# First combine tile of a soft-MoE layer: batch 1's first lower half ahead of the row maxima, and the spreading products between the halves of the lower products

## The chip, the cores and the metric

The kernel runs on 1 core of a Trainium2 chip. The metric is the device time of one execution in microseconds (us). The engines are TensorE (PE; its weight loads are listed as PEld), VectorE (DVE), ScalarE (ACT), GpSimd (POOL) and the DMA queues that SyncE (SP) feeds. Each engine works through its own queue in order, and the engines wait for each other by semaphores.

## What is computed

The program is one layer of attention without softmax (4096 tokens of 256 channels in two batches), a layer norm with residual, then a soft mixture of experts, and another layer norm with residual. The stage of the change is the last one, the combination of the experts' outputs `y`:

```
logits   = einsum("bmd,dnp->bmnp", x, phi)            # 4 x 512 tokens, 64 x 32 = 2048 slots
dispatch = softmax(logits, axis=0)                    # over the batches
combine  = softmax(logits.reshape(b, m, n * p), -1)   # over the 2048 slots of a token
slots    = einsum("bmd,bmnp->bnpd", x, dispatch)
y        = einsum("bnpd,nde->bnpe", slots, W) + b
out      = einsum("bnpd,bmnp->bmd", y, combine)
x        = x + layernorm(out)
```

(The inputs of this case have two batches of 2048 tokens.) The last product is 2 x 2048 tokens by 2048 slots by 256 channels.

## The kernel before

**Stages.** Tokens are cut into 16 tiles of 128 per batch. After attention (to about 100 us) a loop over 16 blocks of slots computes the dispatch products, and from about 370 us the combine stage runs over the 16 tiles, j = 0 to 15. Tile 0 and the step from tile 0 to tile 1 are written out by hand; tiles 2 to 14 are one loop body (`comb_dve(j)` on DVE, `comb_act(j)` on ACT, `comb_pool(j)` on POOL, `next_logits(j + 1)`, `combine(1, j)` and `combine(0, j)` on PE), and the last tile is written out again. PE has a loop of its own from j = 1. There is no scheduler: each engine's order is the order of the code, and semaphores tie them together.

**One tile.** PE forms the 128 x 2048 logits of batch 1 in four banks of psL (96 matmuls, L1706). DVE takes the maximum of each row part (`l_max`, L1307, four times), masks it (`mask1`, L1311), adds the stored difference of the two batches' logits and takes the maxima for batch 0 (`add_max`, L1326, four times), and masks those (`mask0`, L1311 again). A row of 2048 logits lies in four partition quarters, so the masked maxima have to be spread over the partitions: PE multiplies them with a constant (`fold`, L1676, one product for each batch), and DVE makes from the result the bias of the exponential (`exp_bias`, L1332 and L1334). ACT writes `E = exp(...)` for batch 1 and then batch 0 (`exps`, L886, four pieces each). DVE transposes E in two halves (`turn`, L1293), ACT rounds each half to f16 (`hi`, L682), and the rest of the value, a second f16 number, is the "lower half of E": `lo(b, j, half)`, a subtraction on DVE (L1285), or for batch 0's second half on POOL (`lo_second`, L595).

**The combine product.** For each batch, `combine(b, j)` adds up in one bank of psM: 32 upper products (L1724 and L1725 in turn), which need only the rounded E, then 16 lower products (L1728), 8 for each half of E. Before each 8 lower products PE waits for the `lo` of that half (`lows_ready`): for batch 1 both on DVE, for batch 0 in tile 0 in the order second half (`el_pool`, from POOL), first half (`el_ready[0]`, from DVE). In tile 0 (`first`) each of the two `combine` calls also holds one `fold` for tile 1, between its upper and its lower products.

**DVE around the change.** `comb_dve(1, first=True)` is at once the start of tile 1 and the rest of tile 0: in it stand `lo(1, 0, 0)`, `lo(1, 0, 1)` and `lo(0, 0, 0)`, on which PE's lower products of tile 0 wait. It ends with `turns` and `turn` of tile 1 and `lo(1, 1, 0)`, `lo(1, 1, 1)`. `exp_bias(1, 1)` in it makes the bias (`m0_ready`) for ACT's exponentials of batch 0, `exps(0, 1)`. ACT's queue from there is: `exps(0, 1)`, `his(1, 1)`, `u_square`, `u_copy`, `his(0, 1)`. (In `exp_bias` and `lmax` the first argument is 0 for batch 1 and 1 for batch 0; in `lo`, `turn` and `exps` it is the batch.)

In the profile's names, psM and psL are PSUM; xx, r, r_xn and r_y are parts of SBUF (r stands for several tensors with a number), and small holds the statistics.

Of the kernel before, what the change touches and what calls it, by code (L numbers as in the profile page):

```python
# [53 lines left out]
def wait_apart(eng, sem, value):  # L54

    eng.wait_ge(sem, value)
    eng.sem_inc(PASSED[0], 1)
# [33 lines left out]
def build(nc, x, norm_w, norm_b, qkv_w, qkv_b, proj_wT, proj_b, phi, ffn_w, ffn_bT, out):  # L92
# [26 lines left out]
    with ExitStack() as ctx:  # L119
# [3 lines left out]
        def sem(name):  # L123
            return ctx.enter_context(nc.semaphore(name))
# [98 lines left out]
        def per_token():  # L223
# [79 lines left out]
        l_done, m1_ready, m0_ready = sem("l_done"), sem("m1_ready"), sem("m0_ready")  # L303
        l_added = sem("l_added")
        m1_masked, m0_masked, m1_folded, m0_folded = (
            sem("m1_masked"), sem("m0_masked"), sem("m1_folded"), sem("m0_folded"))
# [43 lines left out]
        FOLD = [bk[w][:, 288:288 + EP * GJ] for w in range(2)]  # L350
# [632 lines left out]
        def _(dve):  # L983
# [279 lines left out]
            def y_lo(i):  # L1263
                b, h = y_lots[i]
                t4 = slice(4 * h, 4 * h + 4)
                dve.wait_ge(yh_ready, i + 1)
                if h < 2:
                    V.scalar_tensor_tensor(yl0[:, b, t4], yf[:, b, t4, :], sg[:, 1:2], yh0[:, b, t4, 0:C],
                                           ALU.mult, ALU.subtract).then_inc(yl_ready, 1)
                else:  # L1270
                    u4 = slice(4 * h - 8, 4 * h - 4)
                    V.scalar_tensor_tensor(yhl1[:, b, u4, YC:YC + C], yf[:, b, t4, :], sg[:, 1:2], yhl1[:, b, u4, 0:C],
                                           ALU.mult, ALU.subtract).then_inc(yl_ready, 1)
# [9 lines left out]
            def lo(b, j, half):  # L1283
                dve.wait_ge(eh_ready[b], 2 * j + 1 + half)
                V.tensor_tensor(eT[b][:, 1, 8 * half:8 * half + 8, :].rearrange("p t m -> p (t m)"),  # L1285
                                ET[b][:, 1024 * half:1024 * half + 1024],
                                eT[b][:, 0, 8 * half:8 * half + 8, :].rearrange("p t m -> p (t m)"),
                                ALU.subtract).then_inc(el_ready[b], 1)

            def turn(b, j, half):  # L1290
                dve.wait_ge(E_ready[b], 4 * j + 2 * half + 2)
                g2 = slice(2 * half, 2 * half + 2)
                V.transpose(ET[b].rearrange("p (t g r) -> p g t r", g=GJ, r=Q)[:, g2],  # L1293
                            E[b].rearrange("p (g t c) -> p g t c", g=GJ, c=Q)[:, g2]).then_inc(ET_ready[b], 1)

            def turns(b, j):

                dve.wait_ge(eh_ready[b], 2 * j)
                if b:
                    dve.wait_ge(el_ready[1], 2 * j)  # L1300
                else:
                    dve.wait_ge(el_ready[0], j)
                    dve.wait_ge(el_pool, j)

            def l_max(j, g):
                dve.wait_ge(l_done, 4 * j + g + 1)
                own.add(V.tensor_reduce(lmax[:, 0, g:g + 1], logits_at(j)[:, 512 * g:512 * g + 512], AX_X, ALU.max))  # L1307
# [6 lines left out]
            def mask1():  # L1314

                own.wait()
                mask(0, m1_masked)

            def mask0(j):

                dve.wait_ge(l_added, 4 * j + 4)
                mask(1, m0_masked)

            def add_max(j, g):
                c = slice(512 * g, 512 * g + 512)
                V.tensor_tensor_reduce(E0[:, c], logits_at(j)[:, c], dB[:, c], 1.0, -3.0e38, ALU.add, ALU.max,  # L1326
                                       lmax[:, 1, g:g + 1]).then_inc(l_added, 1)

            def exp_bias(w, j, bank, folded, done):

                dve.wait_ge(folded, j + 1)
                own.add(V.tensor_reduce(m1[:, w], bank.rearrange("p (q g) -> p g q", q=EP), AX_X, ALU.max))  # L1332
                own.wait()
                V.tensor_scalar(ebias[:, w], m1[:, w], kap[:, 1:2], E_LOG, ALU.mult, ALU.add).then_inc(done, 1)  # L1334

            def comb_dve(j, first=False, last=False):
                for g in range(GJ):
                    l_max(j, g)
                mask1()
                if first:  # L1340
                    lo(1, 0, 0)
                    lo(1, 0, 1)
                dve.wait_ge(ET_ready[0], 2 * j)
                wait_apart(dve, dB_loaded, 16 * j + 16)
                add_max(j, 0)
                add_max(j, 1)
                if first:
                    exp_bias(0, j, FOLD[1], m1_folded, m1_ready)
                    y_lo(7)
                add_max(j, 2)  # L1350
                add_max(j, 3)
                if not first:
                    exp_bias(0, j, FOLD[1], m1_folded, m1_ready)
                mask0(j)
                lo(0, j - 1, 0)
                exp_bias(1, j, FOLD[0], m0_folded, m0_ready)
                turns(1, j)
                turn(1, j, 0)
                turn(1, j, 1)
                turns(0, j)  # L1360
                turn(0, j, 0)
                if not last:
                    turn(0, j, 1)
                lo(1, j, 0)
                lo(1, j, 1)
                if last:
                    turn(0, j, 1)
# [25 lines left out]
            turn(0, 0, 1)  # L1393
            y_lo(6)
            comb_dve(1, first=True)
            with dve.Fori(2, NJ - 1) as j:
                own.enter(j - 2, 6)
                comb_dve(j)
                own.leave(NJ - 3)
            comb_dve(NJ - 1, last=True)  # L1400

            lo(0, NJ - 1, 0)
# [36 lines left out]
        def _(pe):  # L1439
# [233 lines left out]
            def fold(w, j, dst, masked, folded):  # L1673

                pe.wait_ge(masked, j + 1)
                mm(dst, w_fold[:, :], fmax[:, w].rearrange("p q g -> p (q g)"), start=True, stop=True).then_inc(folded, 1)  # L1676
# [46 lines left out]
            def high(b, t, acc, first):  # L1723
                mm(acc, eT[b][:, 0, t, :], yh(b, t), start=first, stop=False)  # L1724
                mm(acc[:, 0:C], eT[b][:, 0, t, :], yl(b, t), start=False, stop=False)  # L1725

            def low(b, t, acc, last):
                return mm(acc, eT[b][:, 1, t, :], yh(b, t), start=False, stop=last)  # L1728

            def lows_ready(b, j, half, last):  # L1730

                if b:
                    pe.wait_ge(el_ready[1], 2 * j + half + 1)
                elif half and last:
                    pe.wait_ge(el_ready[0], NJ + 1)
                else:
                    pe.wait_ge(el_pool if half else el_ready[0], j + 1)

            def combine(b, j, seq, more, first=False):

                acc = bk[3 - b][:, 0:C + 1]
                if first:
                    pe.wait_ge(E1_ready, 4)
                    pe.wait_ge(m0_masked, 1)
                    pe.wait_ge(zcol_ready, 3)
                else:
                    pe.wait_ge(u_copied, seq - 1)
                pe.wait_ge(eh_ready[b], 2 * j + 1)
                for t in range(NT):
                    if first and t in (0, 8, 12):  # L1750
                        pe.wait_ge(yl_ready, {0: 4, 8: 6, 12: 8 - b}[t])
                    if t == 4 and more and not b and not first:
                        fold(1, j + 1, FOLD[0], m0_masked, m0_folded)
                    if t == 8:
                        pe.wait_ge(eh_ready[b], 2 * j + 2)
                    high(b, t, acc, t == 0)
                if more and (b or first):
                    fold(1 - b, j + 1, FOLD[b], (m0_masked, m1_masked)[b], (m0_folded, m1_folded)[b])
                order = list(range(NT))
                if first and not b:  # L1760
                    order = order[8:] + order[:8]
                for t in order:
                    if t % 8 == 0:
                        lows_ready(b, j, t // 8, not more)
                    ins = low(b, t, acc, t == order[-1])
                ins.then_inc(comb_done, 1)
# [37 lines left out]
            for kb in range(4):  # L1804
                pe.wait_ge(y_out, 2 + (NB - 1) * TB + kb + 1)
                logits(1, kb, xxT[:, 0, 1])
            combine(1, 0, 0, True, True)
            combine(0, 0, 1, True, True)
            with pe.Fori(1, NJ - 1) as j:
# [36 lines left out]
```

## Time and profile before

| | us |
|---|---|
| median of 3 runs | 638.39 |
| lowest, highest | 637.76, 638.48 |
| the profiled execution, its own time | 637.81 |
| its span, first to last instruction | 635.8 |
| busy in the span: PE, DVE, ACT, POOL | 626.3, 453.9, 359.2, 219.1 |
| mean granted TensorE clock | 0.998 |

Rows of the trace carry times in us from the first instruction. In the timeline of an engine a row is one instruction, or several of one kind in a row with their count (x4); what stands in brackets is the idle time of the engine just before, and what ended it. Consecutive matmuls overlap in the listing: one row of 0.27 us follows the other at 0.11 us. In the table of stretches each engine's busy time stands with the number of its instructions, then the granted clock as a share of full speed.

### The profile page before, as it was taken

What the parts mean: (1) busy time and instruction counts of PE and PEld (TensorE: products, weight loads), DVE (VectorE), ACT (ScalarE), POOL (GpSimd) and SP (SyncE); (2) the same over time, 40 slices, a digit from 0 to 9 for tenths busy, and PEclk for the clock granted to TensorE, in tenths of its full rate; (3) what the DMA queues carried; (4) which work ended last, traced back from release to release, by engine and by line L of the source; (5) the groups of instructions that cost most, each with busy time, mean ns of one, the idle gap of its engine ahead of it and who ended that gap; (6) DMA issues with size and microseconds to landing.
All of it is one profiled execution on the core that took longest, in us unless ns stands there. A gap on an engine that the chain in (4) does not pass through costs nothing.

```text
span 635.8 us, 15342 instructions
## 1 busy us (share of the span) xinstructions
PE 626.3 (98%) x5351; PEld 394.7 (62%) x5351; DVE 453.9 (71%) x899; ACT 359.2 (56%) x694; POOL 219.1 (34%) x376
## 2 busy tenths in 40 slices
PE   8999999999999999999999999999999999999996
PEld 8898645445444444444444456777777777777775
DVE  6988999835433544446243499999888888888886
ACT  5766867642332332323444366777766666666664
POOL 5445866520000000000000001565555555555554
PEclk9999999999999999999999999999999999999999
DMA  8910032325666566655465521222222222222201
GB/s 285 400 65 1 19 66 50 67 55 162 202 197 201 161 187 179 194 174 166 135 174 159 173 78 68 92 91 91 91 91 91 91 91 91 91 91 91 91 16 34
DMA packets 78772, 77.07 MB, mean 121 GB/s; under 512 B 6417, under 2 KB 75282, under 8 KB 76434
## 3 DMA queue, kind: packets, MB, share of 16 engines
q1 hardware_dynamic: 76256, 74.34, 38.3%
q10 hardware_dynamic: 2482, 2.29, 1.1%
q8 instruction: 19, 0.31, 0.2%
q14 instruction: 15, 0.12, 0.1%
HBM read 51.71 MB, written 23.07 MB: 118 GB/s over the span
## 4 chain that ended last, share of the span: by engine, by line
PE 88%; DVE 8%; issue 2%; POOL 1%; ACT 1%; POOLq 0%; DVEq 0%; ACTq 0%
PE psL L1587 26%; PE psM L1574 12%; PE psL L1706 11%; PE psM L1724 7%; PE psM L1728 7%; PE psM L1725 7%; PE psM L1604 4%; PE psL L1474 3%; PE psM L1532 2%; PE psL L1792 1%; PE psM L1481 1%; PE psL L1532 1%; PE psM L1537 1%; DVE r_y L1120 1%; DVE small L1307 1%
## 5 line engine op out<-in xcount | busy, mean ns | idle before, releaser
L1587 PE MATMUL psL<-r,r_xn 128*128 128x512 f16 x768 | 176.3, 379 | 1.3 <-DVE r L1129 1.3
L1587 PEld LDWEIGHTS psL<-r,r_xn 128*128 128x128 f16 x768 | 73.4, 98 | 91.8 <-issue 6.7
L773 ACT ACTIVATE r<-psM,small 128x512 f32<-128x512 f32 x64 | 43.8, 684 | 100.3 <-PE psM L1574 100.3
L1574 PE MATMUL psM<-phs,xx 128*128 128x512 f16 (+1 forms) x384 | 93.2, 379 | 0.3 <-DVE xx L1166 0.3
L590 POOL MEMSET r_xn<- 128x8 f16 x2 | 0.3, 139 | 230.9 <-PE psL L1587 230.9
L1127 DVE TENSOR_SCALAR r<-r 128x512 f16<-128x512 f32 x64 | 28.1, 439 | 70.0 <-ACT r L773 69.8
L1706 PE MATMUL psL<-phs,r 128*32 128x512 f16 x1344 | 75.1, 379 | 0.0
L506 POOL TENSOR_TENSOR small<-small,epst 128x2 f32<-128x2 f32 (+3 forms) x77 | 60.3, 784 | 19.6 <-DVE small L1153 11.8
L1574 PEld LDWEIGHTS psM<-phs,xx 128*128 128x128 f16 x384 | 37.4, 98 | 45.1 <-issue 1.1
L886 ACT ACTIVATE r<-psL,small 128x512 f32<-128x512 f32 x60 | 41.9, 776 | 37.7 <-DVE small L1334 37.4
L1706 PEld LDWEIGHTS psL<-phs,r 128*32 128x32 f16 x1344 | 34.6, 97 | 36.5 <-issue 3.0
L886 ACT ACTIVATE r_xn<-r_xn,small 128x512 f32<-128x512 f32 x64 | 47.1, 824 | 1.3 <-DVE small L1334 1.3
L1129 DVE SCALAR_TENSOR_TENSOR r<-r 128x512 f16<-128x512 f32 x64 | 46.1, 721 | 2.2
L607 POOL TENSOR_SCALAR small<-small 128x1 f32<-128x1 f32 x30 | 20.5, 683 | 69.6 <-ACT r L921 69.2
L1307 DVE TENSOR_REDUCE small<-psL 128x1 f32<-128x512 f32 x60 | 38.2, 683 | 6.0 <-PE psL L1706 6.0
L682 ACT ACTIVATE r<-psM 128x512 f32<-128x512 f32 (+1 forms) x67 | 39.2, 586 | 4.5 <-PE psM L1630 3.2
L1293 DVE STREAM_TRANSPOSE xx<-r_xn 128x1024 f32<-128x1024 f32 x32 | 39.1, 1227 | 2.3 <-ACT r_xn L886 1.5
L1326 DVE CUSTOM_DVE_ANT_0 r_xn<-psL,xx 128x512 f32<-128x512 f32 x60 | 37.9, 687 | 1.7 <-issue 0.6
L595 POOL TENSOR_TENSOR r<-xx,r 128x1024 f16<-128x1024 f32 x15 | 32.0, 2136 | 19.8 <-DVE r_xn L1285 19.8
L1293 DVE STREAM_TRANSPOSE r<-r 128x1024 f32<-128x1024 f32 x32 | 38.1, 1224 | 0.5 <-ACT r L886 0.4
L1253 DVE TENSOR_TENSOR r_y<-psM,r 128x512 f32 (+1 forms) x12 | 8.3, 692 | 40.8 <-PE psM L1604 40.8
L1285 DVE TENSOR_TENSOR r_xn<-r,r_xn 128x1024 f16<-128x1024 f32 x32 | 37.2, 1202 | 0.1
(203 smaller groups left out, 1256.2 us busy)
## 6 DMA issues: line engine op xcount, KB each, us to landing
r<-in_ffn_w SPq DMA_DIRECT2D x23, 1024.0 KB, 5.8
logit_difference<-r SPq DMA_DIRECT2D x256, 64.0 KB, 1.9
xx<-logit_difference SPq DMA_DIRECT2D x16, 1024.0 KB, 4.8
out<-r SPq DMA_DIRECT2D x32, 128.0 KB, 1.7
xres<-in_x SPq DMA_DIRECT2D x6, 512.0 KB, 10.0
r<-in_phi SPq DMA_DIRECT2D x1, 2048.0 KB, 15.6
expert_bias<-r ACTq DMA_DIRECT2D x1, 2048.0 KB, 20.4
r<-expert_bias SPq DMA_DIRECT2D x16, 128.0 KB, 5.4
```

Source lines behind the costliest of these rows:

```text
L506: return nc.gpsimd.tensor_tensor(o, v, epst[:, 0:1].broadcast_to([P, n]), ALU.pow)
L773: nc.scalar.activation(tF[:, j % 2, :], bk[j % 2][:, :], ACT.Tanh, scale=khalf).then_inc(t_ready, 1)
L886: nc.scalar.activation(E[b][:, c], src[:, c], ACT.Exp, bias=ebias[:, w, g:g + 1], scale=kap[:, 0:1]).then_inc(E_ready[b], 1)
L1129: V.scalar_tensor_tensor(thl[:, j % 2, 1], tF[:, j % 2], S_SCALE, thl[:, j % 2, 0], ALU.mult, ALU.subtract).then_inc(s_split, 1)
L1293: V.transpose(ET[b].rearrange("p (t g r) -> p g t r", g=GJ, r=Q)[:, g2], E[b].rearrange("p (g t c) -> p g t c", g=GJ, c=Q)[:, g2]).then_in ...
L1307: own.add(V.tensor_reduce(lmax[:, 0, g:g + 1], logits_at(j)[:, 512 * g:512 * g + 512], AX_X, ALU.max))
L1574: ins = mm(bk[j % 2][:, :].rearrange("p (q m) -> p q m", q=EP), xxT[:, 1, j, hx, k, :], phw[:, hp, k, :, bass.ds(nb, 1), :].rearrange("p q ...
L1587: ins = mm(psL[:, i * 512:(i + 1) * 512], x3n[:, b, j, hx, k * P:(k + 1) * P], thl[:, j % 2, hs, :], start=(j == 0 and hx + hs == 0), stop ...
L1706: ins = mm(logits_at(j)[q * Q:(q + 1) * Q, g * 512:(g + 1) * 512], xj[:, hx, k, g * Q:(g + 1) * Q], phs[:, hp, k, q * 512:(q + 1) * 512], ...
L1724: mm(acc, eT[b][:, 0, t, :], yh(b, t), start=first, stop=False)
L1725: mm(acc[:, 0:C], eT[b][:, 0, t, :], yl(b, t), start=False, stop=False)
L1728: return mm(acc, eT[b][:, 1, t, :], yh(b, t), start=False, stop=last)
```

## The change

On DVE, in the first call of `comb_dve`, `lo(1, 0, 0)` moves ahead of the four `l_max` and `mask1`; `lo(1, 0, 1)` stays behind them. `exp_bias(1, 1)` moves behind the first transpose of batch 1, `turn(1, 1, 0)`. On PE, in the two `combine` calls of tile 0, `fold` moves from ahead of the 16 lower products to between the first 8 and the second 8. Nothing is added or removed, and the loops' bodies keep their order.

```diff
             def comb_dve(j, first=False, last=False):
+                if first:
+                    lo(1, 0, 0)
                 for g in range(GJ):
                     l_max(j, g)
                 mask1()
                 if first:
-                    lo(1, 0, 0)
                     lo(1, 0, 1)
...
                 mask0(j)
                 lo(0, j - 1, 0)
-                exp_bias(1, j, FOLD[0], m0_folded, m0_ready)
+                if not first:
+                    exp_bias(1, j, FOLD[0], m0_folded, m0_ready)
                 turns(1, j)
                 turn(1, j, 0)
+                if first:
+                    exp_bias(1, j, FOLD[0], m0_folded, m0_ready)
                 turn(1, j, 1)
...
-                if more and (b or first):
+                if more and b and not first:
                     fold(1 - b, j + 1, FOLD[b], (m0_masked, m1_masked)[b], (m0_folded, m1_folded)[b])
                 order = list(range(NT))
                 if first and not b:
                     order = order[8:] + order[:8]
                 for t in order:
+                    if first and t == order[8]:
+                        fold(1 - b, j + 1, FOLD[b], (m0_masked, m1_masked)[b], (m0_folded, m1_folded)[b])
                     if t % 8 == 0:
                         lows_ready(b, j, t // 8, not more)
```

PE, the lower products of `combine(1, 0)`, before (L1676 is `fold`, L1728 a lower product):

```order
L1676 MATMUL psM<-small,w_fold 128x16 [waits m1_masked]
L1728 MATMUL psM<-r,r_xn 128x257 [waits el_ready1]
L1728 MATMUL psM<-r,r_xn 128x257 x7
L1728 MATMUL psM<-r_xn 128x257 [waits el_ready1]
L1728 MATMUL psM<-r_xn 128x257 x7
```

The same place now (L1680 is `fold`, L1732 a lower product):

```order
L1732 MATMUL psM<-r,r_xn 128x257 [waits el_ready1]
L1732 MATMUL psM<-r,r_xn 128x257 x7
L1680 MATMUL psM<-small,w_fold 128x16 [waits m1_masked]
L1732 MATMUL psM<-r_xn 128x257 [waits el_ready1]
L1732 MATMUL psM<-r_xn 128x257 x7
```

The fold moved behind the first 8 lower products; in `combine(0, 0)` likewise, where the 8 ahead of it wait for `el_pool`, the 8 behind it for `el_ready0`, and the fold for `m0_masked`.

DVE, the start of `comb_dve(1, first=True)`, as a piece of the difference (L1285 is `lo`, L1307 `l_max`, L1311 `mask1`):

```order
 L1272 SCALAR_TENSOR_TENSOR r_xn<-r_y,small,r_xn 128x4x256
+L1285 TENSOR_TENSOR r_xn<-r,r_xn 128x1024
 L1307 TENSOR_REDUCE small<-psL 128x1 x4
 L1311 TENSOR_TENSOR small<-small 128x16
-L1285 TENSOR_TENSOR r_xn<-r,r_xn 128x1024 x2
+L1285 TENSOR_TENSOR r_xn<-r,r_xn 128x1024
```

One of the two `lo` moved ahead of five instructions; what follows them follows the same set of instructions as before.

DVE, behind `lo(0, 0, 0)` in the same call (L1332 and L1334 are `exp_bias`, L1293 `turn`):

```order
 L1285 TENSOR_TENSOR r<-xx,r 128x1024
-L1332 TENSOR_REDUCE small<-psM 128x4
-L1334 TENSOR_SCALAR small<-small 128x4
-L1293 STREAM_TRANSPOSE r<-r 128x2x16x32 x2
+L1293 STREAM_TRANSPOSE r<-r 128x2x16x32
+L1332 TENSOR_REDUCE small<-psM 128x4
+L1334 TENSOR_SCALAR small<-small 128x4
+L1293 STREAM_TRANSPOSE r<-r 128x2x16x32
 L1293 STREAM_TRANSPOSE xx<-r_xn 128x2x16x32 x2
 L1285 TENSOR_TENSOR r_xn<-r,r_xn 128x1024 x2
```

The bias for ACT's exponentials of batch 0 stands one transpose later.

## Rows read from the trace of the kernel before

**Rows 1.** Stretches: length, busy PE, PEld, DVE, ACT, POOL, clock, DMA share, GB/s

```profile
392.25:408.89 16.64, 16.53 (x197) 12.02 (x196) 15.51 (x27) 12.42 (x25) 9.34 (x15) 1.00 0.33 127
408.89:425.20 16.31, 16.31 (x201) 12.07 (x204) 14.92 (x26) 12.40 (x24) 9.07 (x15) 1.00 0.26 97
```

**Rows 2.** Timeline of DVE, late in the combine stage

```profile
599.77 0.17 DVE L1332 TENSOR_REDUCE small<-psM 128x4 f32<-128x16 f32 x1 [1.14 <-PE psM L1676]
```

**Rows 3.** Timeline of PE, tile 0: folds and lower products

```profile
383.49 0.29 PE L1676 MATMUL psM<-small,w_fold 128*128 128x16 f32 x2
384.12 1.07 PE L1728 MATMUL psM<-r,r_xn 128*128 128x257 f16 x8 [0.34 <-DVE r_xn L1285]
385.26 1.05 PE L1728 MATMUL psM<-r_xn 128*128 128x257 f16 x8
...
389.56 0.27 PE L1725 MATMUL psM<-r_xn,r 128*128 128x256 f16 x1
390.11 0.39 PE L1676 MATMUL psM<-small,w_fold 128*128 128x16 f32 x2 [0.28 <-DVE small L1311]
390.36 1.04 PE L1728 MATMUL psM<-r_xn,r 128*128 128x257 f16 x8
391.25 1.07 PE L1728 MATMUL psM<-r 128*128 128x257 f16 x8
```

**Rows 4.** Timeline of DVE, from the row maxima to the next tile's maxima

```profile
380.24 2.48 DVE L1307 TENSOR_REDUCE small<-psL 128x1 f32<-128x512 f32 x4
...
382.85 2.35 DVE L1285 TENSOR_TENSOR r_xn<-r,r_xn 128x1024 f16<-128x1024 f32 x2
...
389.98 1.22 DVE L1285 TENSOR_TENSOR r<-xx,r 128x1024 f16<-128x1024 f32 x1
...
391.45 2.36 DVE L1293 STREAM_TRANSPOSE r<-r 128x1024 f32<-128x1024 f32 x2
393.74 2.33 DVE L1293 STREAM_TRANSPOSE xx<-r_xn 128x1024 f32<-128x1024 f32 x2
395.99 2.32 DVE L1285 TENSOR_TENSOR r_xn<-r,r_xn 128x1024 f16<-128x1024 f32 x2
398.23 2.48 DVE L1307 TENSOR_REDUCE small<-psL 128x1 f32<-128x512 f32 x4
400.74 0.17 DVE L1311 TENSOR_TENSOR small<-small 128x16 f32<-128x16 f32 x1
```

**Rows 5.** Timeline of ACT, the exponentials of batch 0 and what follows

```profile
391.58 2.93 ACT L886 ACTIVATE r_xn<-r_xn,small 128x512 f32<-128x512 f32 x4 [0.34 <-DVE small L1334]
394.42 1.99 ACT L682 ACTIVATE r_xn<-r 128x1024 f16<-128x1024 f32 x2
```

**Rows 6.** Timeline of PE, tile 1: the two folds

```profile
401.07 0.30 PE L1676 MATMUL psM<-small,w_fold 128*128 128x16 f32 x2
401.22 1.05 PE L1728 MATMUL psM<-r,r_xn 128*128 128x257 f16 x8
...
404.14 0.40 PE L1676 MATMUL psM<-small,w_fold 128*128 128x16 f32 x2
404.38 0.27 PE L1724 MATMUL psM<-r 128*128 128x257 f16 x1
```

**Rows 7.** Timeline of DVE: the biases and the maxima's mask

```profile
386.54 0.90 DVE L1334 TENSOR_SCALAR small<-small 128x4 f32<-128x4 f32 x1
...
403.77 0.23 DVE L1334 TENSOR_SCALAR small<-small 128x4 f32<-128x4 f32 x1
403.90 0.18 DVE L1311 TENSOR_TENSOR small<-small 128x16 f32<-128x16 f32 x1
```

**Rows 8.** Timeline of POOL

```profile
385.28 2.13 POOL L595 TENSOR_TENSOR r<-xx,r 128x1024 f16<-128x1024 f32 x1 [19.77 <-DVE r_xn L1285]
...
397.11 1.34 POOL L607 TENSOR_SCALAR small<-small 128x1 f32<-128x1 f32 x1 [5.48 <-ACT r L921]
...
401.75 2.14 POOL L595 TENSOR_TENSOR r<-xx,r 128x1024 f16<-128x1024 f32 x1
```

## The prediction

> **What bounds the kernel now.** I read the table of stretches first, because the share of busy time over the whole span mixes stages. In the combine stage a tile costs PE about 16.3 us, and in the stretch 408.89 to 425.20 PE is busy for all 16.31 us of it; the stretch before it, 392.25 to 408.89, is 0.33 us longer with 0.11 us idle in it [rows 1]. So from the third tile on PE alone sets the pace. The timeline of DVE late in the stage says the same from the other side: DVE stands idle 1.14 us until PE's fold comes [rows 2]. Whatever PE loses or gains in the first two tiles is therefore carried to the end unchanged: nothing later has slack to give it back, and nothing later eats it.
>
> In tile 0, where the change is, it is different. The reader should look at PE's lower products and at what released them [rows 3]. In `combine(1, 0)` the fold starts at 383.49, the first 8 lower products at 384.12, the second 8 at 385.26. Eight lower products take 0.89 us (390.36 to 391.25), so PE waits twice, once named (0.34 on L1285). Both waits are for `lo` on DVE: the pair of them runs from 382.85 to 385.20 [rows 4], and 385.26 is 0.06 behind its end. In `combine(0, 0)` the upper products end at about 389.67 (the last record starts at 389.56, and they follow each other by 0.11), the fold starts at 390.11 behind DVE's mask L1311, and the last 8 lower products start at 391.25 [rows 3]. The `lo(0, 0, 0)` they need runs from 389.98 for 1.22, to 391.20 [rows 4]. That is 0.05 ahead of them: they start as early as DVE lets them, even though 8 products happen to stand in between. The chain that matters in tile 0 is DVE's own queue.
>
> **The change part by part.** The sum is made against the profiled execution's own time, 637.81.
>
> *1. `lo(1, 0, 0)` ahead of the maxima.* DVE starts it at 380.24, when `l_max` started before [rows 4]; one costs half of the distance of a pair to its successor, (398.23 - 395.99) / 2 = 1.12. It ends at about 381.4, long before PE wants it at 383.49. The maxima and the mask shift by 1.12, and `lo(1, 0, 1)` comes behind them. The set of instructions up to its end is the same, so it ends at 385.20 as before, and the second 8 lower products still start at 385.26. Gain of PE: 0. The first wait is gone, and the second grows by as much.
>
> *2. The fold behind the first 8 lower products in `combine(1, 0)`.* PE does the 8 from 383.49 to 384.38, then the fold. The mask is 1.12 later than before, at about 384.05, so the fold does not wait; unwaited it takes 0.15 (401.07 to 401.22) [rows 6] and ends at 384.53. DVE reads its result for the bias at 386.54 [rows 7], so this is hidden with about 1.9 to spare; without that cover `m1_ready` would slip. Then PE waits until 385.26. Cost 0.
>
> *3. The fold in `combine(0, 0)`.* The 8 products on `el_pool` need POOL's subtraction, 385.28 plus 2.13 = 387.41 [rows 8]; they go at 389.67 and end at 390.56. The fold follows without its wait of before (the mask allowed it at 390.11) and ends at 390.71. Then the last 8 wait for `lo(0, 0, 0)` until 391.25 or 391.26. Gain 0, at most 0.01 of loss. `next_logits` follows at 392.25 as before. The bounds of parts 1 to 3 together: between 383.49 and 386.15 (385.26 plus 0.89) PE has 16 products and a fold, 1.93 of work in 2.66, and between 389.67 and 392.14 the same in 2.47. So the idle time to be had is 0.73 + 0.54 = 1.27 us; no gain can be larger. I take 0, since DVE's order leaves both ends where they are.
>
> *4. `exp_bias(1, 1)` behind a transpose.* This is the only part with a price. DVE's transpose costs (393.74 - 391.45) / 2 = 1.15 [rows 4]. The bias comes that much later. ACT was idle 0.34 waiting for exactly this bias, before it began batch 0's exponentials at 391.58 [rows 5]; it now begins at 392.73. DVE gains nothing, since its sum is the same. But DVE's transposes of batch 0 need these exponentials: the second pair is complete at 392.73 + 2.93 = 395.66 [rows 5], so the last transpose starts at about 395.71, where it had started at 393.74 + 1.13 = 394.87 [rows 4]. DVE is late by 0.84. The first of the two waits as well (its two pieces are ready at about 394.2) but is done by 395.4, inside that. Next in ACT's queue is `his(1, 1)`, 394.42 + 1.15 = 395.57, with 1.99 for both [rows 5]: the halves are there at about 396.6 and 397.56, before DVE's `lo` of tile 1 wants them at 396.83 and 397.95. No second delay. ACT's own lag of 1.15 is taken up further on: its next exponentials wait for a bias of DVE anyway.
>
> *5. Where it reaches PE.* DVE's maxima of tile 2 start at 399.07, not 398.23, and their mask ends at 400.74 + 0.17 + 0.84 = 401.75 [rows 4]. PE was at its fold at 401.07, with no slack worth naming: the mask had been done at 400.91. Now the fold waits to 401.81 and, waited for, costs 0.25 as at 404.14, not 0.15 [rows 6]; the lower products begin at 402.06, not 401.22: 0.84 late. The other fold, at 404.14, starts 0.06 behind its mask (403.90 + 0.18) [rows 7], so it waited for DVE already; with DVE 0.84 late it starts at 404.98, while PE arrives at 403.87 + 0.84 = 404.71. Again 0.84, not added. In the next tile both engines are late alike, and PE runs without a gap.
>
> Sum: 0 + 0 + 0 + 0.84 = **+0.84 us**, 638.65 for the profiled execution. It lies 0.58 under the median, so the forecast is **639.2**. About 0.2% (1.28 us) is what a measurement of this kernel can tell from no change, and 0.84 is 0.13%.
>
> **What could add to it.** The bias's last step, L1334, took 0.90 us at 386.54 and 0.23 at 403.77 [rows 7]. The long one ended at 387.44, and POOL's L595 at 387.41; the short one met the tail of the same POOL instruction, 401.75 + 2.14 = 403.89 [rows 8]. In this trace, then, the tiny instruction stands still while POOL's subtraction runs. The Trainium skill, page "SBUF — State Buffer", section "Who interferes with whom", gives the rule: DVE and GpSimd share a pair of ports as an exclusive lock, which `tensor_scalar` can want, and whoever starts first blocks the other. The trace agrees (0.90 against 0.23). For the second tile the order decides: DVE's L1334 comes at 404.61; POOL's chain to L595 begins with L607, whose 1.34 us ended at 398.45, just behind DVE's pair of `lo` (395.99 + 2.32 = 398.31). That pair ends 0.84 later, so I expect POOL 0.84 later as well, its end at 404.73, and the same brush as before.
>
> **The rivals.**
> *Slower beyond 0.2%.* POOL follows ACT's lag of 1.15 or more rather than DVE's 0.84, so its L595 still holds when L1334 comes; the mask behind L1334, the second fold and all of PE follow. With POOL 0.31 later than assumed this adds 0.2; the full block seen before, 0.90 - 0.23 = 0.67, gives 0.84 + 0.67 = 1.51, that is 639.9. It decides from the point where L595 starts later than 402.7. For it: ACT's u_square releases POOL's chain and is 1.15 late. Against it: POOL waited for DVE there already.
> *No delay at all (-0.1 to +0.3).* The transposes wait less than I say, or PE's fold had more slack than its neighbours show. The 0.06 and 0.16 between masks and folds speak against it. 638.4.
> *Faster.* If DVE were not the end of both waits, up to 1.27 of idle time would fall to PE: 637.1, and 638.0 with the 0.84 paid. It needs `lo(1, 0, 1)` and `lo(0, 0, 0)` to end earlier, and neither has less ahead of it in its queue. That the moves don't take effect is excluded by the order, which shows them.
>
> **How the numbers follow.** Forecast (+0.6 to +1.2) 0.70; POOL rival (+1.2 to +1.6) 0.14; no delay 0.11; faster 0.05. Left out are 0.1 at either end, and runs lie 0.7 apart, so the range is 638.1 to 640.1. Beyond 0.2% slower: the POOL rival and a corner of the forecast, 0.19. Faster beyond 0.2%: 0.04. Within: 0.77.
>
> **What would show it.** Right: PE's lower products of tile 0 start at 385.26 and 391.25 still, with the waits now ahead of the second 8 each time; ACT's batch 0 exponentials start near 392.7; the last transpose has a wait on ACT; the folds of the next tile start near 401.8 and 405.0; the stretch that was 16.64 is 17.5, and the next 16.3. Wrong: if the second 8 start earlier, parts 1 to 3; if the transposes do not wait, part 4; if PE's fold is at 401.1, part 5; if L1334 near 404.6 takes 0.5 or more, the POOL rival.

## The result

The changed kernel takes 638.94 us (median of 22 runs, 638.39 to 639.68), the kernel before 638.12 us (22 runs beside them, 637.55 to 638.70). The ratio is 1.0013, with a 95% interval of 1.0007 to 1.0019: slower by 0.82 us, clear of noise and less than 0.2%.

The two profiled executions differ by more, 637.7 us of span against 635.8, and the first thing to do is to find a place from which they can be compared. DVE's `y_lo(6)`, L1272, is the last instruction ahead of everything that the change moves. (`y_lo(i)` makes the second, lower f16 half of one of eight parts of `y`; the last upper products of `combine(1, 0)` need `y_lo(6)`, those of `combine(0, 0)` need `y_lo(7)`.) The logits of tile 3 on PE are the first work after which PE alone sets the pace. Timelines of DVE and of PE, before:

```profile
379.08 1.25 DVE L1272 SCALAR_TENSOR_TENSOR r_xn<-r_y,small,r_xn 128x1024 f16<-128x1024 f32 x1
```

```profile
408.89 5.36 PE L1706 MATMUL psL<-phs,r 128*32 128x512 f16 x96
```

and after:

```profile
380.06 1.24 DVE L1272 SCALAR_TENSOR_TENSOR r_xn<-r_y,small,r_xn 128x1024 f16<-128x1024 f32 x1
```

```profile
410.70 5.36 PE L1710 MATMUL psL<-phs,r 128*32 128x512 f16 x96
```

From the one to the other it is 408.89 - 379.08 = 29.81 us before and 410.70 - 380.06 = 30.64 us after: **+0.83**. The other 0.98 us were there when the stage began (the last section says where they come from). To set a time of after beside one of before, take 0.98 off. Everything behind this stretch is as long as it was: the last instruction of DVE starts the same distance behind tile 3's logits in both, 633.18 - 408.89 = 634.99 - 410.70 = 224.29. DVE's timelines, before and after:

```profile
633.18 0.48 DVE L1417 SCALAR_TENSOR_TENSOR r<-r,small 128x256 f32<-128x256 f32 x1 [0.41 <-POOL small L506]
```

```profile
634.99 0.48 DVE L1421 SCALAR_TENSOR_TENSOR r<-r,small 128x256 f32<-128x256 f32 x1 [0.41 <-POOL small L506]
```

The table of stretches of after, cut at the starts of the logits (columns as in [rows 1]):

```profile
393.22:410.70 17.48, 16.80 (x197) 12.03 (x196) 15.70 (x29) 13.09 (x25) 9.05 (x15) 1.00 0.34 123
410.70:426.97 16.27, 16.27 (x198) 12.03 (x197) 14.88 (x26) 12.36 (x24) 9.07 (x15) 1.00 0.28 97
```

The stretch that was 16.64 is 17.48, with PE idle for 0.68 in it, and the next one has no idle time at all [rows 1]. PE's timeline of after, where [rows 3] and [rows 6] were:

```profile
384.47 1.06 PE L1732 MATMUL psM<-r,r_xn 128*128 128x257 f16 x8
385.37 0.29 PE L1680 MATMUL psM<-small,w_fold 128*128 128x16 f32 x2
386.24 1.05 PE L1732 MATMUL psM<-r_xn 128*128 128x257 f16 x8 [0.58 <-DVE r_xn L1285]
...
390.65 1.04 PE L1732 MATMUL psM<-r_xn,r 128*128 128x257 f16 x8
391.53 0.29 PE L1680 MATMUL psM<-small,w_fold 128*128 128x16 f32 x2
392.23 1.07 PE L1732 MATMUL psM<-r 128*128 128x257 f16 x8 [0.40 <-DVE r L1285]
...
402.79 0.40 PE L1680 MATMUL psM<-small,w_fold 128*128 128x16 f32 x2 [0.58 <-DVE small L1311]
403.03 1.05 PE L1732 MATMUL psM<-r,r_xn 128*128 128x257 f16 x8
...
405.94 0.40 PE L1680 MATMUL psM<-small,w_fold 128*128 128x16 f32 x2
```

The reader should see two things. In tile 0 both folds run without a wait, and behind each one PE now waits longer for `lo`: the second 8 lower products start at 386.24 and 392.23, less 0.98 at 385.26 and 391.25, the very times of [rows 3]. And the fold of the next tile has a wait of 0.58 for DVE's mask that was not there [rows 6].

DVE's timeline of after, from the split pair of transposes on:

```profile
392.09 1.24 DVE L1293 STREAM_TRANSPOSE r<-r 128x1024 f32<-128x1024 f32 x1
...
393.42 0.23 DVE L1334 TENSOR_SCALAR small<-small 128x4 f32<-128x4 f32 x1
393.56 1.24 DVE L1293 STREAM_TRANSPOSE r<-r 128x1024 f32<-128x1024 f32 x1
395.33 2.56 DVE L1293 STREAM_TRANSPOSE xx<-r_xn 128x1024 f32<-128x1024 f32 x2 [0.54 <-ACT r_xn L886]
397.81 2.31 DVE L1285 TENSOR_TENSOR r_xn<-r,r_xn 128x1024 f16<-128x1024 f32 x2
400.05 2.47 DVE L1307 TENSOR_REDUCE small<-psL 128x1 f32<-128x512 f32 x4
402.56 0.18 DVE L1311 TENSOR_TENSOR small<-small 128x16 f32<-128x16 f32 x1
...
405.58 0.23 DVE L1334 TENSOR_SCALAR small<-small 128x4 f32<-128x4 f32 x1
```

and ACT's beside it:

```profile
393.68 2.93 ACT L886 ACTIVATE r_xn<-r_xn,small 128x512 f32<-128x512 f32 x4 [1.47 <-DVE small L1334]
396.52 1.99 ACT L682 ACTIVATE r_xn<-r 128x1024 f16<-128x1024 f32 x2
```

ACT's wait for the bias went from 0.34 [rows 5] to 1.47. Then DVE waits for ACT: 0.54 ahead of the first transpose of batch 0, and some more inside the pair, which takes 397.81 - 395.33 = 2.48 to its successor instead of 2.25 [rows 4].

### The profile page after: what moved, and what is told of

It is laid out like the page before. It is cut to its first block, busy times and chain, and to the rows that moved or that the text cites. A ratio compares the mean times of both kernels' runs of the same rounds, so it can differ in the third digit from the quotient of the medians.

```text
span 637.7 us, 15342 instructions
## 1 busy us (share of the span) xinstructions
PE 627.2 (98%) x5351; PEld 395.9 (62%) x5351; DVE 454.0 (71%) x899; ACT 359.5 (56%) x694; POOL 218.8 (34%) x376
## 4 chain that ended last, share of the span: by engine, by line
PE 88%; DVE 8%; issue 2%; ACT 1%; POOL 1%; POOLq 0%; DVEq 0%; ACTq 0%
PE psL L1591 25%; PE psM L1578 12%; PE psL L1710 11%; PE psM L1728 7%; PE psM L1732 7%; PE psM L1729 7%; PE psM L1608 4%; PE psL L1478 3%; PE psM L1536 2%; PE psL L1798 1%; PE psM L1485 1%; PE psL L1536 1%; PE psM L1541 1%; DVE r_y L1120 1%; DVE small L1307 1%
## 5 line engine op out<-in xcount | busy, mean ns | idle before, releaser
L607 POOL TENSOR_SCALAR small<-small 128x1 f32<-128x1 f32 x30 | 20.2, 673 | 70.7 <-ACT r L921 70.4
L1307 DVE TENSOR_REDUCE small<-psL 128x1 f32<-128x512 f32 x60 | 38.2, 682 | 6.1 <-PE psL L1710 6.1
L682 ACT ACTIVATE r<-psM 128x512 f32<-128x512 f32 (+1 forms) x67 | 39.2, 586 | 4.8 <-PE psM L1634 3.2
L1293 DVE STREAM_TRANSPOSE xx<-r_xn 128x1024 f32<-128x1024 f32 x32 | 39.3, 1229 | 2.9 <-ACT r_xn L886 2.1
L595 POOL TENSOR_TENSOR r<-xx,r 128x1024 f16<-128x1024 f32 x15 | 32.1, 2138 | 19.8 <-DVE r_xn L1285 19.8
L1293 DVE STREAM_TRANSPOSE r<-r 128x1024 f32<-128x1024 f32 x32 | 38.2, 1225 | 0.5 <-ACT r L886 0.4
L1285 DVE TENSOR_TENSOR r_xn<-r,r_xn 128x1024 f16<-128x1024 f32 x32 | 37.2, 1200 | 0.1
```

## The experiments

Each kernel was timed 11 times (e3_bias_later 8 times) beside the kernel before on the same chip. Most of the differences are below what separates one execution from the next, so the table also gives the distance in the trace from the start of `y_lo(6)` to the start of tile 3's logits, read as above. Each distance is from one trace; where two kernels should not differ, they agree to 0.02 (before and e1_bias_back, after and e2_bias_only). Behind tile 3's logits, to the start of DVE's last instruction, it is 224.27 to 224.30 in all but the last kernel, e8_copy_after.

| kernel | y_lo(6) | logits of tile 3 | distance | to before | median, before beside it | ratio (95%) |
|---|---|---|---|---|---|---|
| before | 379.08 | 408.89 | 29.81 | | | |
| after | 380.06 | 410.70 | 30.64 | +0.83 | 638.94, 638.12 | 1.0013 (1.0007 to 1.0019) |
| e1_bias_back | 379.94 | 409.73 | 29.79 | -0.02 | 638.58, 638.41 | 1.0000 (0.9991 to 1.0009) |
| e2_bias_only | 379.78 | 410.42 | 30.64 | +0.83 | 639.22, 638.41 | 1.0014 (1.0005 to 1.0023) |
| e3_bias_later | 379.67 | 411.43 | 31.76 | +1.95 | 640.24, 638.41 | 1.0029 (1.0018 to 1.0039) |
| e4_both_lo | 380.11 | 409.63 | 29.52 | -0.29 | 637.60, 638.41 | 0.9991 (0.9982 to 1.0000) |
| e5_early_bias | 380.25 | 409.79 | 29.54 | -0.27 | 638.05, 638.40 | 0.9994 (0.9985 to 1.0003) |
| e6_early_and_late | 379.77 | 409.75 | 29.98 | +0.17 | 638.36, 638.40 | 1.0000 (0.9991 to 1.0009) |
| e7_all_ahead | 379.06 | 408.37 | 29.31 | -0.50 | 637.78, 638.04 | 0.9991 (0.9982 to 1.0000) |
| e8_copy_after | 380.22 | 409.50 | 29.28 | -0.53 | 638.07, 638.04 | 0.9999 (0.9990 to 1.0008) |

**The late bias undone.** Against the changed kernel:

```diff
-                if not first:
-                    exp_bias(1, j, FOLD[0], m0_folded, m0_ready)
+                exp_bias(1, j, FOLD[0], m0_folded, m0_ready)
                 turns(1, j)
                 turn(1, j, 0)
-                if first:
-                    exp_bias(1, j, FOLD[0], m0_folded, m0_ready)
                 turn(1, j, 1)
```

> The changed kernel with the bias of batch 0 (exp_bias(1, 1)) back at its old place; lo(1, 0, 0) ahead of the maxima and both folds between the lower products stay. My theory (the whole loss comes from the later bias, the other moves only shift PE's waits): 0.0 us against the kernel before, at most 0.1 either way, with PE's second 8 lower products 1.77 us apart from their start as before and the fold of the next tile again within 0.1 us of its place. Rival (the folds between the lower products or the moved lo cost the time themselves): +0.3 to +0.8 us stays. Rival (these moves gain, and the bias hid it): -0.3 to -1.2 us.

Measured: 1.0000, and -0.02 us in the trace. PE's timeline:

```profile
386.12 1.06 PE L1729 MATMUL psM<-r_xn 128*128 128x257 f16 x8 [0.58 <-DVE r_xn L1285]
...
392.10 1.07 PE L1729 MATMUL psM<-r 128*128 128x257 f16 x8 [0.40 <-DVE r L1285]
...
401.92 0.29 PE L1677 MATMUL psM<-small,w_fold 128*128 128x16 f32 x2
```

The waits behind the folds are those of after, 0.58 and 0.40, and they cost nothing; the fold of the next tile waits for nothing. So the moved `lo` and the moved folds together neither gain nor lose.

**The late bias alone.** Against the kernel before:

```diff
-                exp_bias(1, j, FOLD[0], m0_folded, m0_ready)
+                if not first:
+                    exp_bias(1, j, FOLD[0], m0_folded, m0_ready)
                 turns(1, j)
                 turn(1, j, 0)
+                if first:
+                    exp_bias(1, j, FOLD[0], m0_folded, m0_ready)
                 turn(1, j, 1)
```

> The kernel before with one edit: exp_bias(1, 1) behind the first transpose of batch 1. My theory: +0.8 us, ACT's exponentials of batch 0 start 1.15 later behind the bias, the last transposes of DVE wait about 0.5 and 0.3 us for them, the mask and the fold of the next tile are 0.84 late. Rival (the loss needs the moved folds as well): 0 to +0.3 us.

Measured: 1.0014, +0.83 us in the trace, the whole loss, as expected. DVE's transposes and PE's fold:

```profile
395.05 2.56 DVE L1293 STREAM_TRANSPOSE xx<-r_xn 128x1024 f32<-128x1024 f32 x2 [0.54 <-ACT r_xn L886]
```

```profile
402.51 0.40 PE L1679 MATMUL psM<-small,w_fold 128*128 128x16 f32 x2 [0.58 <-DVE small L1311]
```

**The bias later still**, behind both transposes of batch 1:

```diff
-                exp_bias(1, j, FOLD[0], m0_folded, m0_ready)
+                if not first:
+                    exp_bias(1, j, FOLD[0], m0_folded, m0_ready)
                 turns(1, j)
                 turn(1, j, 0)
                 turn(1, j, 1)
+                if first:
+                    exp_bias(1, j, FOLD[0], m0_folded, m0_ready)
```

> The kernel before with exp_bias(1, 1) behind both transposes of batch 1, so the bias is 2.29 us late instead of 1.15. My theory: ACT begins batch 0's exponentials at 391.58 + 2.29 = 393.87 of the old trace, their fourth ends at 396.80, the last transpose starts at 396.85 instead of 394.87: DVE and behind it PE 2.0 us late. Rival (DVE's or PE's slack takes up a fixed part, or the loss is a fixed cost of splitting the pair of transposes): +0.8 to +1.2 us as with one transpose, or less.

Measured: 1.0029, +1.95 us in the trace, where 2.0 was expected. ACT, DVE and PE in turn:

```profile
394.42 2.93 ACT L886 ACTIVATE r_xn<-r_xn,small 128x512 f32<-128x512 f32 x4 [2.60 <-DVE small L1334]
```

```profile
396.07 2.55 DVE L1293 STREAM_TRANSPOSE xx<-r_xn 128x1024 f32<-128x1024 f32 x2 [1.69 <-ACT r_xn L886]
```

```profile
403.52 0.40 PE L1679 MATMUL psM<-small,w_fold 128*128 128x16 f32 x2 [1.49 <-DVE small L1311]
```

The second transpose of delay costs 1.95 - 0.83 = 1.12 us, nearly its own length of 1.15 [rows 4], while the first cost 0.83: the first 0.3 us of lateness are hidden by what DVE still had to do ahead of its transposes of batch 0, and nothing is hidden after that. A fixed cost of splitting the pair is ruled out, since here the pair stands together.

**Both `lo` ahead of the maxima.** If DVE's queue is what counts in tile 0, the 0.67 us that its L1334 loses there [rows 7] should be worth more than any wait of PE. Against the kernel before:

```diff
+                if first:
+                    lo(1, 0, 0)
+                    lo(1, 0, 1)
                 for g in range(GJ):
                     l_max(j, g)
                 mask1()
-                if first:
-                    lo(1, 0, 0)
-                    lo(1, 0, 1)
```

with PE's fold of `combine(1, 0)` behind its 16 lower products and that of `combine(0, 0)` between them.

> Both lo(1, 0, 0) and lo(1, 0, 1) ahead of the row maxima, the fold of combine(1, 0) behind all its 16 lower products, the fold of combine(0, 0) between its halves, the bias at its old place. My theory: PE's two waits in combine(1, 0) go (about 0.7 us), POOL's subtraction starts 2.6 us earlier and is over before DVE's small bias instruction L1334, which then takes 0.23 us instead of 0.90, so DVE's queue is 0.67 us shorter; the fold of the next tile is reached about 0.7 us earlier: -0.7 us against the kernel before. Rival (DVE's queue up to the next tile's mask is what counts and the lock of POOL does not go or comes back elsewhere): 0 us, with the waits of PE moved on to combine(0, 0) or the next tile's folds.

Measured: 0.9991, but -0.29 us in the trace, well short of -0.7. DVE, POOL and PE:

```profile
386.05 0.57 DVE L1311 TENSOR_TENSOR small<-small 128x16 f32<-128x16 f32 x1
...
387.96 0.23 DVE L1334 TENSOR_SCALAR small<-small 128x4 f32<-128x4 f32 x1
```

```profile
384.46 2.13 POOL L595 TENSOR_TENSOR r<-xx,r 128x1024 f16<-128x1024 f32 x1 [17.93 <-ACT r L682]
```

```profile
386.68 0.40 PE L1676 MATMUL psM<-small,w_fold 128*128 128x16 f32 x2 [0.22 <-DVE small L1311]
```

L1334 is free, 0.23. But POOL did not start 2.6 us earlier, as I had put it, only 1.85 (4.35 behind `y_lo(6)` instead of 6.20): its subtraction also needs ACT's rounded half, and the row names ACT L682 as its releaser. So it ran to 386.59, over DVE's mask1, which took 0.57 instead of 0.18: the lock moved from one small instruction to another, and 0.67 - 0.39 = 0.28 of the gain was left. The mechanism of the rival in the expectation held, a lock that comes back elsewhere, though not its 0 us.

**The bias of batch 1 ahead of POOL's release.** Against the kernel before:

```diff
                 if first:
                     lo(1, 0, 0)
+                    exp_bias(0, j, FOLD[1], m1_folded, m1_ready)
                     lo(1, 0, 1)
...
-                if first:
-                    exp_bias(0, j, FOLD[1], m1_folded, m1_ready)
-                    y_lo(7)
                 add_max(j, 2)
                 add_max(j, 3)
                 if not first:
                     exp_bias(0, j, FOLD[1], m1_folded, m1_ready)
                 mask0(j)
+                if first:
+                    y_lo(7)
```

> The kernel before with DVE's bias of batch 1, exp_bias(0, 1), moved up from behind two of the four additions to between lo(1, 0, 0) and lo(1, 0, 1), that is ahead of the release of POOL's subtraction, and y_lo(7) moved back behind the additions and mask0. My theory: L1334 of that bias takes 0.23 us instead of 0.90, no instruction of DVE that needs the port falls into POOL's 2.13 us, DVE reaches the maxima of the next tile 0.7 to 0.8 us earlier, neither fold of the next tile waits, and PE gains 0.2 in combine(0, 0) and 0.37 at the second fold: -0.55 us, counted from y_lo(6) on in the trace. Rival (the lock comes back on another instruction, as on mask1 in e4_both_lo): -0.1 to -0.3 us. Rival (PE's highs now wait for y_lo(7)): 0 or slower.

Measured: 0.9994, -0.27 us in the trace, half of the -0.55 expected. DVE, POOL and PE:

```profile
385.36 0.23 DVE L1334 TENSOR_SCALAR small<-small 128x4 f32<-128x4 f32 x1
```

```profile
386.80 2.14 POOL L595 TENSOR_TENSOR r<-xx,r 128x1024 f16<-128x1024 f32 x1 [20.11 <-DVE r_xn L1285]
```

```profile
390.62 0.28 PE L1724 MATMUL psM<-r_xn,r 128*128 128x257 f16 x1 [0.15 <-DVE r_xn L1272]
...
391.52 0.29 PE L1676 MATMUL psM<-small,w_fold 128*128 128x16 f32 x2
```

The lock is gone, and DVE's queue is 0.67 shorter: `lo(0, 0, 0)`, ahead of which the same instructions stand, starts at 390.48, which is 10.23 behind `y_lo(6)` instead of 389.98 - 379.08 = 10.90. More than half of that is lost on PE: its first row is an upper product that waits for `y_lo(7)`, which I had let PE reach with nothing to spare. With that, PE itself ends last, and the fold that DVE's next bias needs, in the second row, comes late as well: that bias starts 1.37 behind `lo(0, 0, 0)`, at 391.85, instead of 1.13 (391.11 - 389.98 in the kernel before).

**The same kernel with the late bias of the change.**

> e5_early_bias with the late bias of the changed kernel (exp_bias(1, 1) behind the first transpose of batch 1). My theory: the price of the late bias is not a constant, it is what is left after DVE's and PE's slack. DVE is about 0.75 us earlier here, of which PE uses 0.57, so some 0.2 us of the lag is covered, and ACT's exponentials start some 0.2 earlier than DVE's gain alone says: the price against e5 is 0.4 to 0.65 us, and the kernel stands at -0.15 to +0.1 us against the kernel before, where in the changed kernel it was +0.84. Rival (a fixed price): +0.84 against e5, +0.3 against the kernel before.

Measured: 1.0000, +0.17 us in the trace, so 0.44 us against the kernel without it. That price lies in the expected 0.4 to 0.65; against the kernel before it is more than the expected +0.1, because e5_early_bias had gained less than expected. The very same edit costs 0.83 in one kernel and 0.44 in another. DVE's named wait for ACT is unchanged, 0.54. But the bias had waited for PE's fold in e5_early_bias, and one transpose later it does not, so DVE's `lo` of tile 1 come only 0.61 later (17.09 behind `y_lo(6)` instead of 16.48), not 0.84. The rest of the cover is on PE, because DVE had been ahead of it: the first fold of tile 1 starts 22.09 behind `y_lo(6)` in both kernels, and only the second, below, is late, by 0.34; the other 0.10 is in the two folds, which take longer to their successors (0.22 and 0.25 instead of 0.15).

```profile
394.38 2.56 DVE L1293 STREAM_TRANSPOSE xx<-r_xn 128x1024 f32<-128x1024 f32 x2 [0.54 <-ACT r_xn L886]
```

```profile
404.99 0.39 PE L1679 MATMUL psM<-small,w_fold 128*128 128x16 f32 x2
```

**Everything that needs the port ahead of the maxima.** The last two kernels put the lessons together. Against the kernel before, on DVE (PE's fold of batch 1 goes to the middle of the upper products of `combine(0, 0)`, that of batch 0 between its lower halves):

```diff
+                if first:
+                    lo(1, 0, 0)
+                    lo(1, 0, 1)
+                    y_lo(7)
                 for g in range(GJ):
                     l_max(j, g)
                 mask1()
-                if first:
-                    lo(1, 0, 0)
-                    lo(1, 0, 1)
...
                     exp_bias(0, j, FOLD[1], m1_folded, m1_ready)
-                    y_lo(7)
```

Measured: 0.9991 (637.78 against 638.04), -0.50 us in the trace, more than the -0.3 to -0.4 expected. DVE, POOL and ACT:

```profile
386.20 0.18 DVE L1311 TENSOR_TENSOR small<-small 128x16 f32<-128x16 f32 x1
...
387.83 0.23 DVE L1334 TENSOR_SCALAR small<-small 128x4 f32<-128x4 f32 x1
```

```profile
383.43 2.33 POOL L595 TENSOR_TENSOR r<-xx,r 128x1024 f16<-128x1024 f32 x1 [17.94 <-ACT r L682]
```

```profile
391.34 2.94 ACT L886 ACTIVATE r_xn<-r_xn,small 128x512 f32<-128x512 f32 x4
```

POOL's subtraction runs beside the four maxima, and both small instructions are free. Batch 0's exponentials start 12.28 behind `y_lo(6)` instead of 12.50, 0.22 earlier where 0.1 was expected. The ACT row has no idle time ahead of it any more: ACT now sets when batch 0's exponentials begin. That suggested one more step.

```diff
             def comb_act(j):
                 exps(1, j, False)
-                u_copy(1, 2 * j - 2)
                 exps(0, j, False)
+                u_copy(1, 2 * j - 2)
```

> e7_all_ahead with ACT's u_copy of batch 1 behind batch 0's exponentials in every tile of the loop, so that ACT has 0.5 us less ahead of them. My theory: ACT's queue was the last thing in the way of the gain in e7; now the last transpose of DVE waits for nothing, and from y_lo(6) to the logits of tile 3 it is -0.7 us, all of DVE's lock time. Rival (something else ends last, in DVE or PE): no more than e7.

Measured: 0.9999, -0.53 us in the trace, 0.03 more than e7 where some 0.2 more was expected (-0.7). (`u_copy` takes the finished product of the tile before out of PSUM; POOL's work for the layer norm follows it.) The exponentials do start earlier, and DVE's second mask hardly moves:

```profile
392.15 2.93 ACT L886 ACTIVATE r_xn<-r_xn,small 128x512 f32<-128x512 f32 x4
```

```profile
404.51 0.17 DVE L1311 TENSOR_TENSOR small<-small 128x16 f32<-128x16 f32 x1
```

Counted from `y_lo(6)` they begin at 11.93 us instead of 12.28, and DVE's second mask at 24.29 instead of 24.33 (403.39 - 379.06, the mask of e7). So ACT was only just behind DVE's queue in e7, and what ends last is that queue itself: 24.82 before [rows 7], 24.29 now, 0.53 of the 0.67 of the lock. Of the rest, 0.1 is in tile 0: the first mask is now followed by an addition, which starts 0.19 to 0.20 behind it (387.35 to 387.55 in e8), where the `lo` of the kernel before started 0.10 behind it (382.75 to 382.85). Another 0.04 is in the pair of `lo` of tile 1, which takes 2.28 to its successor instead of 2.24.

Behind tile 3's logits e8 loses more than the 0.03 that it gained over e7. DVE's last instruction in e7 and in e8:

```profile
632.67 0.48 DVE L1417 SCALAR_TENSOR_TENSOR r<-r,small 128x256 f32<-128x256 f32 x1 [0.41 <-POOL small L506]
```

```profile
634.05 0.48 DVE L1417 SCALAR_TENSOR_TENSOR r<-r,small 128x256 f32<-128x256 f32 x1 [0.41 <-POOL small L506]
```

It starts 632.67 - 408.37 = 224.30 behind them in e7 and 634.05 - 409.50 = 224.55 in e8. From `y_lo(6)` to the end e8 is thus 0.22 slower than e7 (253.83 against 253.61), and only 0.27 faster than the kernel before (254.10). The edit is in the loop's body, so it also puts off the copy in every later tile; in the last tile POOL's and ACT's steps of the layer norm come 0.25 late (ACT's L972 at 629.78 - 409.50 = 220.28 instead of 628.40 - 408.37 = 220.03), while PE's last products are 0.04 late. Which step of the later tiles carries the delay stays open.

The ratios of e4 and e7 touch 1.0000 with the upper end of their intervals, so that they are faster is shown by the traces rather than by the times. The medians of e8 and e7 lie 0.29 apart, near the 0.22 of the whole traces, but their intervals overlap.

## Why the prediction was right

The forecast was 639.2 with +0.84 for the change; measured were 638.94 and +0.82, and +0.83 in the trace. The 0.26 between the two absolute times lie in the median that it started from, 638.39 of 3 runs, where 22 runs gave 638.12. The prediction took 0.2% (1.28 us) as what a measurement can tell from no change; the 22 runs of each told 0.13% apart.

*Parts 1 to 3, nothing gained or lost.* Right, and shown by e1_bias_back (-0.02). The second 8 lower products start at 385.26 and 391.25 once the 0.98 are taken off, as said. Both edits took away a wait that the next instruction on PE had to make anyway, since `lo(1, 0, 1)` and `lo(0, 0, 0)` end when DVE's queue lets them.

*Part 4, the late bias.* Right in mechanism and size. ACT started at 392.70 (said 392.73), DVE waited ahead of the first transpose and again inside the pair, and its `lo` of tile 1 came at 396.83 (said 396.83). Shown by e2_bias_only as the whole loss, and by e3_bias_later as a price that grows nearly one for one beyond a cover of some 0.3 us (1.12 for 1.13 more of lateness at ACT).

*Part 5, the way to PE.* Right: the folds stand at 401.81 and 404.96 (said 401.8 and 404.98), the delays are not added, and no later stretch gives anything back.

*The POOL rival.* It did not come: POOL's L595 and DVE's L1334 moved together. POOL's timeline of after:

```profile
399.21 1.05 POOL L607 TENSOR_SCALAR small<-small 128x1 f32<-128x1 f32 x1 [6.61 <-ACT r L921]
...
403.56 2.14 POOL L595 TENSOR_TENSOR r<-xx,r 128x1024 f16<-128x1024 f32 x1
```

Less 0.98, L595 starts at 402.58 (said 402.59, deciding point 402.7), and L1334 took 0.23 at 405.58. L607 again ended just behind DVE's pair of `lo`, 400.26 against 397.81 + 2.31 = 400.12, although it began 1.40 behind that pair's start instead of 1.12: it was shorter by as much, 1.05 instead of 1.34; the same line takes 0.27 at 405.68. So ACT's lag did reach the start of L607, as the rival said, but its end went by DVE. The page "SBUF — State Buffer" of the Trainium skill, in "Who interferes with whom", says that a DVE instruction with two SBUF inputs contends with a GpSimd instruction that reads SBUF, and that the one that comes first holds the shared ports until it ends; these two ends agree with it, 0.14 behind each time.

*What the prediction left unsaid*: that the same lock costs the kernel before 0.67 us in its own tile 0, on the one queue that has no slack. It used the 0.90 of L1334 only as a danger of the change. e4, e5 and e7 show that its order can be changed for a gain of up to 0.5 us.

## What to carry to other kernels

Before a wait is removed, ask what the waiting engine needs next and which queue delivers that; if it is the same queue in the same order, the wait only moves. An instruction that feeds another engine is dear to put off, however short it is: here some 0.3 us of DVE's time, moved behind one transpose, made ACT idle, ACT made DVE idle, and PE paid 0.83. The price of such a move holds only for the slack around it (0.83 in one kernel, 0.44 in another), so it has to be worked out anew whenever the neighbours change.

## What the runs showed of the hardware that was not expected

**Most of the spread between the profiled executions is made in the first 8 us.** The stage begins between 379.06 and 380.25 us in the ten profiled executions, whatever the kernel. PE's first block, the 14 warm-up products (28 records), before:

```profile
1.91 5.19 PE L1537 MATMUL psM<-r 128*128 128x128 f32 x28 [1.91 <-POOL r L482]
```

and after:

```profile
1.90 6.17 PE L1541 MATMUL psM<-r 128*128 128x128 f32 x28 [1.90 <-POOL r L482]
```

6.17 - 5.19 is 0.98, the whole offset between the two traces. Over all ten the block takes 4.92 to 6.34 us: e7, the shortest with 4.92, has the earliest `y_lo(6)`, e5, the longest with 6.34, the latest. From the start of the products that follow the block to `y_lo(6)` it is 372.13 to 372.40, so up to 0.27 arises later. The block runs at two rates: its records start at 5 to 7 per us at first, and at 10 or 11 per us from 5 to 6 us on in e7 and from 6 to 7 us on in the kernel before; in all others they are still at 7 there. So it is the time of the change of rate that differs. The granted clock is listed as 1.00 in that stretch in each of them, so these rows don't say what changes the rate. A difference of a few tenths of a microsecond is better read from a place in the trace behind it than from medians.

**Small instructions of DVE stand still behind a large one of POOL.** 128x4 took 0.90 instead of 0.23 in the kernel before, 128x16 with two inputs 0.57 instead of 0.18 in e4; each ended 0.03 us behind POOL's subtraction. DVE's maxima, which read PSUM, and its additions of PSUM and SBUF did not become longer beside it (2.48 for four maxima in e7, as in [rows 4]; 0.69 for an addition beside it and 0.68 without in the kernel before). It goes the other way too: in e5 POOL's 128x1 L602 took 0.89 instead of the 0.19 of the kernel before; it ended at 391.75, 0.05 behind DVE's `lo(0, 0, 0)`.

**An awaited fold costs more than its wait.** From its start to the next product it takes 0.14 to 0.15 when its mask was ready well before, and 0.24 to 0.25 when PE has waited for it ([rows 6] and the same rows of the other kernels). Three folds lie between, with 0.19 to 0.22: the first of tile 1 in e6, e7 and e8, where the mask had ended only 0.07 to 0.10 ahead, against 0.15 or more in the free ones of that place.
